# Attention kernel on one core: the outputs of a unit's eight key blocks in three runs instead of four

## The reference

```python
xn = _layernorm(x)                                   # x: (8, 1024, 512), float32
q, k, v = (heads(xn @ W.T + b) for W, b in ...)      # 16 heads of 32
scores = q @ k.T / sqrt(32)
im = arange(1024) % 256
scores = where(im[:, None] >= im[None, :], scores, -1e30)
attn = softmax(scores) @ v
s = merge(attn) @ Wo.T + bo
y = clip((xn @ sign(Wf).T) * scale + bias, -100, 100)
out = x + s * silu(y)
```

## Time and profile before

| what | value |
|---|---|
| three runs | 1747.96, 1748.41, 1748.90 us; median 1748.41 us |
| profiled execution, its own time | 1749.87 us |
| its span, first to last instruction | 1748.0 us |
| instructions | 34003 |

### The profile page before, as it was taken

One profiled execution on the slowest core, in us unless ns is written; L12 is line 12 of the kernel. 1 busy time (PEld: TensorE's weight loads), 2 busy tenths in 40 slices (PEclk: granted clock), 3 DMA queues, 4 the chain that ended last, 5 costly groups with the idle time before them and its releaser, 6 DMA issues.

```text
span 1748.0 us, 34003 instructions
## 1 busy us (share of the span) xinstructions
PE 1682.2 (96%) x11652; PEld 777.4 (44%) x11652; DVE 1320.4 (76%) x2620; ACT 1220.3 (70%) x2854; POOL 1160.3 (66%) x1154
## 2 busy tenths in 40 slices
PE   8999999999999999999999999999999999999978
PEld 3443444444444444444444444444444444444323
DVE  6888678787678777787777867788677886688772
ACT  4587776776667766678766777657776677676774
POOL 0067666775867667775578855688656776767763
PEclk9999999999999999999999999999999999999989
DMA  7314311343124322243122431224212342122111
GB/s 202 114 38 86 73 44 50 98 91 75 37 62 106 92 50 56 64 104 84 38 74 62 109 78 29 74 74 104 68 44 56 92 86 60 34 62 73 44 50 49
DMA packets 185038, 126.09 MB, mean 72 GB/s; under 512 B 106912, under 2 KB 159264, under 8 KB 184416
## 3 DMA queue, kind: packets, MB, share of 16 engines
q1 hardware_dynamic: 183904, 123.13, 28.0%
q10 hardware_dynamic: 960, 0.79, 0.2%
HBM read 41.50 MB, written 17.05 MB: 33 GB/s over the span
## 4 chain that ended last, share of the span: by engine, by line
PE 76%; ACT 16%; DVE 4%; issue 3%; POOL 1%; ACTq 0%; DMA 0%; SPq 0%; DVEq 0%; POOLq 0%
PE pJ L488 26%; PE pO L692 14%; PE pS L649 10%; PE pT L673 9%; ACT pS L808 6%; PE pT L669 3%; PE pJ L580 3%; ACT PT L796 3%; PE pJ L581 3%; PE pJ L584 3%; PE pS L652 2%; ACT acc L796 2%; DVE mx L1008 1%; PE pT L633 1%; ACT xs L719 1%
## 5 line engine op out<-in xcount | busy, mean ns | idle before, releaser
L1008 DVE TENSOR_REDUCE mx<-pS 128x1 f32<-128x512 f32 (+3 forms) x1216 | 780.2, 656 | 292.3 <-PE pS L649 190.7
L796 ACT ACTIVATE PT<-pT 128x512 f32<-128x512 f32 (+1 forms) x1092 | 637.5, 594 | 413.1 <-PE pT L673 366.9
L1177 POOL TENSOR_TENSOR acc<-acc,PT 128x512 f32<-128x512 f32 x620 | 756.5, 1256 | 37.8 <-PE pO L692 37.8
L673 PE MATMUL pT<-QK 97*128 97x512 f16 (+3 forms) x1280 | 393.0, 318 | 17.6 <-ACT acc L796 10.9
L649 PE MATMUL pS<-QK 96*128 96x512 f16 (+3 forms) x1280 | 391.9, 319 | 16.5 <-ACT pS L808 10.5
L808 ACT ACTIVATE pS<-pS,a 128x384 f32<-128x384 f32 (+3 forms) x512 | 277.0, 547 | 8.3 <-DVE a L1023 8.0
L692 PE MATMUL pO<-PT,V 128*32 128x512 f32 (+3 forms) x2824 | 265.1, 487 | 0.6
L488 PE MATMUL pJ<-xT,wh_q 128*128 128x512 f16 x512 | 192.6, 381 | 1.9 <-ACT xT L737 1.5
L669 PE MATMUL pT<-QK 128*128 128x128 f16 x1024 | 180.9, 220 | 13.1 <-ACT PT L796 10.1
L488 PE MATMUL pJ<-wh_v,xT 128*128 128x512 f16 x512 | 192.1, 378 | 0.8 <-ACT V L776 0.8
L649 PEld LDWEIGHTS pS<-QK 96*128 96x128 f16 x1280 | 124.1, 97 | 154.4 <-ACT pS L808 35.4
(11 more groups left out here) (161 smaller groups left out, 2342.7 us busy)
## 6 DMA issues: line engine op xcount, KB each, us to landing
QK<-sg SPq DMA_DIRECT2D x756, 64.0 KB
xs<-in_x SPq DMA_DIRECT2D x60, 256.0 KB, 3.1
xr<-in_x SPq DMA_DIRECT2D x58, 256.0 KB, 3.1
out<-xr SPq DMA_DIRECT2D x58, 256.0 KB, 2.5
QK<-aT SPq DMA_DIRECT2D x256, 1.0 KB, 1.7
rq<-moved SPq DMA_DIRECT2D x132, 2.0 KB, 1.7
QK<-in_x SPq DMA_DIRECT2D x8, 256.0 KB, 4.4
QK<-in_mqk SPq DMA_DIRECT2D x2, 512.0 KB, 10.1
```

The costliest lines, as they stand in the source:

```text
L673: ins = e.matmul(slot[:, to:to + 512 - q0], k4[0:97, j, kc], q4[0:97, j, q0:512], start=True, stop=True)
L796: e.activation(probabilities_at(i), t_bank("t", i)[:, 0:cols], ACT.Exp, scale=SS).then_inc(s_p, 1)
L1008: e.tensor_reduce(mx[:, par, part, :].rearrange("p (j q) -> p j q", q=4)[:, heads[0]:heads[-1] + 1, qi], s_bank("s", i)[:, 0:cols].rearran ...
L1177: e.tensor_tensor(a, a, PT[:, RING_AT[i] % NPT, 0:width * len(heads)].rearrange("p (j q) -> p j q", j=len(heads)), ALU.add).then_inc(s_ap, 1)
```

## The change

The planner gets a table of runs, `RUNS`. Even units keep (0, 1), (2, 3). Odd units have (0, 1, 2), (3, 4), (5, 6, 7): three runs. The instructions and the semaphores are the same; only their order in each engine's list changes. Block 0's outputs stand four tiles later in TensorE's list than before. Besides, most of the planner's offsets are set anew, by fractions of a step to a few steps.

```diff
-                CHUNKS.append((38 * (_n // 2 - 1) + ((3 + 1.4 * _k) if _n % 2 == 0 else (18.3 + 0.82 * _k)),
+                CHUNKS.append((38 * (_n // 2 - 1) + ((3 + 1.4 * _k) if _n % 2 == 0 else (19.38 + 0.82 * _k)),
...
+RUNS = ((range(0, 2), range(2, 4)), (range(0, 3), range(3, 5), range(5, 8)))
+
+
 def at_pv(n, kb):
 
-    return at_t(T_LAST[n, kb | 1]) + 1.44 + 0.01 * (kb & 1)
+    run = next(r for r in RUNS[n % NQS] if kb in r)
+    return at_t(T_LAST[n, run[-1]]) + 1.44 + 0.01 * (kb - run[0])
 
 
 def at_sums(n):
 
-    return at_pv(n + 1, 1) + 0.01 if n not in ROW_AT else at_pv(n, 4 * (n % NQS) + 3) - -1.17
+    return at_pv(n + 1, RUNS[0][0][-1]) + 0.01 if n not in ROW_AT else at_pv(n, 4 * (n % NQS) + 3) - -1.17
...
 def wish(kind, a, b):
...
-        return 4 * SL * a + (-97.65, -93.55, -92.31, -87.5, -63.31, -75.95, -58.02, -57.58)[b]
+        return 4 * SL * a + (-97.65, -93.03, -92.31, -87.5, -64.98, -72.19, -60.25, -57.58)[b]
...
-        first = x0 + (-50.92 if b == 1 else -88.73)
-        return first, first + 4.56, 0.59, first + 15.16
-    return x0 + -14.94, x0 + -15.33, 0.49, x0 + -5.64
+        first = x0 + (-50.46 if b == 1 else -86.7)
+        return first, first + 4.56, 0.59, first + 15.82
+    return x0 + -14.41, x0 + -15.33, 0.49, x0 + -5.64
...
             def additions():
                 for k, i in enumerate(ADD_V):
-                    yield at_t(i) + 8.42
+                    yield at_t(i) + 9.11
...
             def layer_norm():
-                    yield at_ln(hb)[1] + 0.7
+                    yield at_ln(hb)[1] + 1.2
...
             def additions():
                 for k, i in enumerate(ADD_P):
-                    yield at_t(i) + 2.75
+                    yield at_t(i) + 3.35
```

More of the change, by code:

```diff
@@ L145, in wish @@
     if kind == "qk":
-        return SL * (a - 2) + ((4.3, 15.37, 17.61, 18.51), (5.34, 14.91, 15.83, 22.48), (4.76, 13.8, 14.88, 22.56), (5.13, 12.64, 16.14, 20.67))[a % NG][b]
+        return SL * (a - 2) + ((4.3, 15.37, 17.52, 18.51), (5.34, 14.91, 17.27, 22.48), (4.24, 13.8, 14.88, 22.56), (5.13, 13.32, 16.14, 20.67))[a % NG][b]
     if kind == "v" and a == 0:
-        return -54.64 + 4.88 * b if b < 2 else -33.05 + 9.77 * (b - 2)
+        return -54.64 + 4.88 * b if b < 2 else -33.05 + 9.64 * (b - 2)
     if kind == "v":
-        return 4 * SL * a + (-75.68, -66.09, -61.15, -46.54, -45.38, -33.95, -27.33, -16.49)[b]
+        return 4 * SL * a + (-74.81, -63.75, -61.15, -46.3, -45.38, -34.91, -27.33, -16.49)[b]
     if kind == "f" and a == B - 1:
-        return 4 * SL * B + (-99.65, -74.84, -71.47, -63.0, -50.39, -47.49, -37.14, -23.8)[b]
+        return 4 * SL * B + (-100.44, -74.84, -71.47, -63.0, -47.5, -47.49, -37.14, -24.58)[b]
     if kind == "f":
-        return 4 * SL * (a + 1) + (-18.65, -8.82, 1.47, 12.19, 23.24, 24.32, 37.86, 46.91)[b]
+        return 4 * SL * (a + 1) + (-18.65, -8.82, 1.47, 12.78, 23.24, 24.32, 37.86, 46.91)[b]
     if kind == "o" and a == B - 1:
-        return 4 * SL * B + (-20.46 + 4.2 * b if b < 4 else -4.06 + 3.56 * (b - 4))
+        return 4 * SL * B + (-20.46 + 4.2 * b if b < 4 else -4.06 + 3.23 * (b - 4))
     if kind == "o":
-        return 4 * SL * (a + 1) + (-8.68, -1.88, 8.27, 20.34, 36.36, 39.53, 41.48, 58.21)[b]
+        return 4 * SL * (a + 1) + (-8.68, -1.88, 8.27, 22.59, 36.36, 39.53, 43.83, 58.21)[b]
     return 3.85
-LEN = {"x": 0.33, "sm": 0.4, "qk": 3.52, "v": 3.3, "f": 2.46, "o": 3.28, "b": 3.0}
+LEN = {"x": 0.33, "sm": 0.4, "qk": 3.49, "v": 3.3, "f": 2.46, "o": 3.28, "b": 3.0}
 PJ, PJ_ORDER, PJ_INDEX = {}, [], {}
@@ L209, in at_gate @@
     first = past("f", *divmod(i, NT)) + 0.5
-    return first + (0, -0.58, 2, 4.84, 5.5)[k] / 5.5 * min(4.74, past_o(i) + 0.3 - first)
+    return first + (0, -1.37, 2, 4.84, 5.5)[k] / 5.5 * min(4.65, past_o(i) + 0.3 - first)
 def at_ln_first(i):
-    return (FIRST + (-5.01, -3.3, -2.77, -2.2, 0.5, 0.85, 2.15, 3.08)[i],
-            FIRST + (-2.37, -2.1, 2.95, 3.17)[i // 2],
-            FIRST + (-0.53, -0.32, 0.01, 0.14, 4.73, 4.52, 6.43, 5.6)[i])
+    return (FIRST + (-5.01, -3.47, -3.01, -2.2, 0.18, 0.85, 2.15, 2.96)[i],
+            FIRST + (-2.43, -1.91, 2.95, 3.17)[i // 2],
+            FIRST + (-0.55, -0.32, 0.01, 0.14, 4.73, 4.52, 6.43, 5.6)[i])
 def at_ln(hb):
@@ L725, in split_x @@
                     i = NT + k
-                    yield at("x", *divmod(i, NT)) - 1.9
+                    yield at("x", *divmod(i, NT)) - 2.07
                     ln.wait_ge(*row_done(i))
@@ L733, in take_xt @@
                     for t in range(NT):
-                        yield past("x", b, t) + -0.02
+                        yield past("x", b, t) + -0.17
                         i = b * NT + t
@@ L871, in split_weights @@
                 for n, (key, i) in enumerate(w_pieces):
-                    yield at_split(n) + ((1.05, 0.36)[n] if n < 2 else 0.5)
+                    yield at_split(n) + ((0.77, 0.36)[n] if n < 2 else 0.5)
                     ln.wait_ge(s_wh, n + 1)
@@ L973, in split_x @@
                     i = NT + k
-                    yield at("x", *divmod(i, NT)) - 0.83
+                    yield at("x", *divmod(i, NT)) - 0.6
                     ln.wait_ge(s_hi, k + 1)
@@ L1028, in shifts @@
                 for m in range(NU):
-                    yield at_s(S_LAST[m]) + 1.47 + 0.16 + (0.43 if m in ROW_AT else 0)
+                    yield at_s(S_LAST[m]) + 1.35 + 0.16 + (0.43 if m in ROW_AT else 0)
                     par = m % 2
@@ L1074, in normalise @@
                 for n in range(NU):
-                    yield past("sm", n) + (-0.45 if n in ROW_AT else 0.04)
+                    yield past("sm", n) + (-0.45 if n in ROW_AT else 0.13)
                     ln.wait_ge(s_on, n)
@@ L1183, in normalise @@
                     s, cs = gn % NSLOT, slice(qs * 512, qs * 512 + 512)
-                    yield past("sm", n) + (0.32 if n in ROW_AT else 0.98)
+                    yield past("sm", n) + (0.81 if n in ROW_AT else 1.18)
                     ln.wait_ge(s_R, n + 1)
@@ L1187, in normalise @@
                     e.tensor_tensor(On[n % 2][:, :], On[n % 2][:, :], R[:, :], ALU.mult).then_inc(s_on, 1)
[L1188 removed]
+                    yield past("sm", n) + (3.84 if n in ROW_AT else 3.17)
                     ln.wait_ge(s_oh, n + 1)
@@ L1291, in move_sums @@
                 for n in ROW:
-                    yield at_s(S_LAST[n]) + (3.78 if n < NU - 1 else 7.0)
+                    yield at_s(S_LAST[n]) + (3.78 if n < NU - 1 else 6.89)
                     par = ROW_AT[n] % 2
```

6 lines of the change are left out of this document (3 added, 3 removed).

## The result

The changed kernel takes 1822.37 us (median of 4, 1821.47 to 1823.56) against 1748.66 us (1747.96 to 1750.71): 1.0417 times as long, 95% interval 1.0405 to 1.0430. It is **slower by 4.2%, 73.7 us**. The sign of the forecast was right, its size was not: 6.6 us were forecast, and the range ended at 1764.

The account below looks back on a forecast made before the run. TensorE, busy in 96% of the span, was taken as the bound. Saved runs (-8.1 us) plus ACT's idling at batch turns (+14.7), other terms 0, gave +6.6 us: median 1755.0 us, range 1740 to 1764.

Parts of the forecast that it names:

- Part 1: TensorE's runs: each costs 0.25 us whatever its length; one fewer in each of 32 odd units saves 8.1 us.
- Part 2, the shift: GpSimd's first addition of an odd unit waits for block 0's outputs, 5.4 us later in unit 19, 4.1 to 4.4 elsewhere.
- Part 2, its price: Cost of the late additions by kind of odd unit: hidden in three kinds, 14.7 us more at batch turns.
- part 4: Other offsets, start and end: reorder work off the path; offsets 0, bounds -3.8 and +3.8; end 0, bounds 0 and 5 us.
- Cost 0: Units 7, 15, 23 ...: late additions cost nothing, covered by POOL's idle time behind them and the 12 PT buffers.
- Costs of 0, 0, 0 and 2.1 us per unit: Late additions' cost in units 5, 13 ..., 7, 15 ..., 1, 9 ... (0 each) and 3, 11 ... at batch turns (2.1).
- The batch turn: Units 3, 11, 19 ... 51: POOL's late layer norm leaves ACT idle 2.1 us before `LN`, seven times, 14.7 us more.
- Part 3: Stretch losing its run, units 7, 15, 23 ...: PE might wait for ACT; moved `LN` activations relieve it; 0, bounds 0 and 13 us.
- Slower by more, 1766: Rival: at batch turns the row sums' 3.6 us hold instead of ACT's 2.1; 1765.5 us, chance 0.08.
- The gain is eaten: Rival: PE saves 8.1 us but waits 7 x 1.1 us behind ACT in the stretch losing its run; 1748 us, chance 0.18.
- the full gain: Rival: the additions' lateness is swallowed everywhere; 1740.3 us, up to 1744.9 with part left; full or nearly full, chance 0.34.

Follow-up runs that it names:

- the version above: Kernel before with runs (0,1), (2,3,4), (5,6,7) only in odd units 3, 7, 11, 15 ... 55, four runs in other odd units, before's offsets: 1743.36 us, ratio 0.9962.

## Why the prediction was right in its sign and wrong in its size

**Part 1 (a run costs 0.25 us): right.** The starts of neighbours give 0.09 and 0.15 us per run again, and there are 160 runs for 192. But that such a saving arrives isn't shown by itself: with long runs in all odd units nothing of it arrives (0.9997), and the version above gains 6 us where fourteen runs are worth 3.5. The estimate of 0.11 us for both ways by the Trainium skill's page ("TensorE: Matmul & The Clock Gate", Step-by-step) stays too low beside them.

**Part 2, the shift: right.** 4.9 us per odd unit in POOL's wait, 4.1 to 5.4 forecast. **Part 2, its price: this is the first step that failed; part 4 is the second, and in the changed kernel the larger one.** I followed the *additions* to their own consumers, the ring of PT buffers and the row sums, and put "Cost 0. The cover is this idle time and the ring of 12 PT buffers". Those two are indeed loose in the changed kernel: the ring's wait went from 23.1 to 21.9 us, the row sums' from 3.8 to 9.5. But idle time *behind* twenty additions covers nothing for what stands *among* them, nor for what another engine does beside them. I didn't ask what else is queued behind the waiting addition, and who waits for that: the gate's `Y` steps are, and ACT's tanh. Nor did I ask which work of VectorE would now run at the same time as the additions: its small steps do, and they are held up. The row that shows how full POOL's list is, 0.32 us idle before unit 25's `Y` at 733.80, stood in the timeline from which the earlier trace rows is taken; I took only the end of the additions from it. Costs of 0, 0, 0 and 2.1 us per unit were forecast, 14.7 us in all. Measured: 108 us with additions alone late and before's offsets; on top of the new offsets, 25 us (1822.4 against 1797.4), the 8 us of the saved runs already taken off.

**The batch turn.** I forecast ACT idle for 2 us before `LN`, released by POOL. ACT never waits for POOL there; all idle time before its `LN` in the whole trace is 2.9 us, three times, and another engine ends it. The kind at the batch turn did lose most (+3.7 us in unit 19), but by maxima that came late behind VectorE's stretched steps (PE idle for 2.14, 0.33 and 0.21 us), by the slow clock behind them and by one wait of 1.51 us for exponentials. The 14.7 us were the right sign for a wrong reason: "slower" hung on this term alone, so the sign was luck.

**Part 3 (the stretch that loses its run): 0 was taken, bounds 0 and 13.** With block 0's outputs early and block 1's late the loss is 14 us, so the upper bound was about right, for before's offsets. In the changed kernel (1.0417), block 0's return brings the old offsets-only ratio (1.0274 in both), so there the part is near 0, as taken.

**Part 4 (the offsets, 0 with bounds of 3.8 us): the second step that failed.** "They reorder work off the path" held for no arrangement: +48 us with the old runs, -38 us with the late ones. I took as the measure of an order PE's wait for late additions, 3.8 us; an order here decides whether POOL, ACT and VectorE meet their times, and where the idle time before a step is 0.3 us, as before `Y`, fractions of a step are enough to miss them. Which of the offsets cost the 48 us was not tried and stays open; that kernel shows PE waiting 40.4 us for ACT's exponentials where before has 16.2.

**The rivals.** "Slower by more, 1766" named the row sums as the place: they are not it. "The gain is eaten" and "the full gain" fell with the sign. None of the rivals had the gate, VectorE's small steps or a price of the offsets beyond 3.8 us, so none could give the size, and the range of 1740 to 1764 was made of terms that all left it out.

## What to carry to other kernels

When an instruction at the head of a run of work on an in-order queue becomes later, the price isn't set by that work's own consumers: list everything between it and the next idle time of the queue, read each one's slack from the idle time before it, and list what other engines do beside the new place of the work. A hand-placed schedule with engines at 66 to 96% has that slack in tenths of a microsecond, and linear losses (58 us for two steps, 107 for four) are the sign that there is none. Don't take a set of offsets for harmless because each moves little: these cost 48 us. And a sum over the whole kernel can hide two effects of opposite sign; split it by kind of unit. Take a saving of fixed costs only in those units where a trace with the cut shows a gain: fourteen of the odd units gave 6 us, all of them gave nothing.

## What the runs showed of the hardware that I had not expected

VectorE's tensor_scalar and tensor_tensor operations of 2 to 16 columns take about 0.17 us alone. Beside GpSimd's operations on 512 columns or 384 (additions, the gate's bias, the results) they took up to 3.7 us in the changed kernel and up to 6.6 us in the one whose additions alone are late. In these two kernels and in the one before, each of the 165 that took over 0.3 us ends within 0.05 us of the end of a GpSimd operation that ran beside it, and a long one spans several of them. The layer norm's first one (L967 after) had a median of 2.77 us in the seven batch turns. Those over 0.3 us come to 26.4 us in 34 operations before, 60.4 in 64 after and 85.4 in 67 with additions alone late; the 280 operations of one column, 128x1, keep their time of about 0.16 us in each. After PE's stop of 2.14 us the clock went to its lower level, 1.2 GHz, for some 3 us of matmuls, so that the wait cost more than its own length.
